# Up matmuls three slots ahead of the down matmuls instead of two, in a fused gated-EMA block and mixture of experts

## The reference

```
# layer 1, per batch
ctx   = ema(x, tau_ctx);  gated = x * sigmoid([x, ctx] @ Wg.T + bg)
mod   = 0.5 + sigmoid(gelu(x @ Wn1.T + bn1) @ Wn2.T + bn2)         # [t, 8]
trace_d = ema(gated * mod[:, d], tau_d), d = 0..7;  temporal = sum_d trace_d * softmax(blend)_d
gate  = sigmoid(temporal @ Wtemp.T + btemp);  soma = gelu(x @ Wsoma.T + bsoma)
x = x + layernorm((soma * gate) @ Wout.T) * gamma + beta
# layer 2, per batch: 3 shared dense blocks, 2 of 4 experts picked by the batch's type
dense(x, wi, wo) = relu(x @ wi) @ wo                               # wi 256x1024, wo 1024x256
s0, s1, s2 = dense(x, shared);  e = wa * dense(x, expert a) + wb * dense(x, expert b)
g = softmax(relu([e, s0, s1, s2](token 0) @ gate_w1) @ gate_w2)
x = x + g0 * e + g1 * s0 + g2 * s1 + g3 * s2
```

## Time and profile before

| | us |
|---|---|
| median of 3 runs | 1072.47 (1072.46 to 1073.15) |
| the profiled execution | 1071.64 |
| its span | 1070.1 |
| TensorE matmul busy | 1049.0 (98%) |
| VectorE busy | 767.1 (72%) |
| ScalarE busy | 398.4 (37%) |
| granted TensorE clock, mean | 0.998 of full |

### The profile page before, as it was taken

One profiled execution on the slowest core, in us unless ns is written; L12 is line 12 of the kernel. 1 busy time (PEld: TensorE's weight loads), 2 busy tenths in 40 slices (PEclk: granted clock), 3 DMA queues, 4 the chain that ended last, 5 costly groups with the idle time before them and its releaser, 6 DMA issues.

```text
span 1070.1 us, 12753 instructions
## 1 busy us (share of the span) xinstructions
PE 1049.0 (98%) x4870; PEld 861.0 (80%) x4870; DVE 767.1 (72%) x1269; ACT 398.4 (37%) x640; POOL 8.9 (1%) x20
## 2 busy tenths in 40 slices
PE   7799999999999999999999999999999999999998
PEld 5388777888788888888888888888888888888898
DVE  7979987499655995469864797539965499545236
ACT  6454445422333333432344323442233323323232
POOL 0000001000000000000000000000000000000000
PEclk9999999999999999999999999999999999999999
DMA  6359888676354574546644565445645456355582
GB/s 221 115 198 411 300 324 308 239 285 267 134 189 158 197 262 141 186 158 252 220 157 158 178 238 195 176 157 213 249 146 181 158 205 246 140 198 195 198 321 91
DMA packets 38142, 223.80 MB, mean 209 GB/s; under 512 B 4482, under 2 KB 5250, under 8 KB 16450
## 3 DMA queue, kind: packets, MB, share of 16 engines
q1 hardware_dynamic: 35778, 210.42, 54.5%
q0 software_dynamic: 2304, 12.58, 3.1%
HBM read 189.30 MB, written 33.69 MB: 208 GB/s over the span
## 4 chain that ended last, share of the span: by engine, by line
PE 57%; DVE 40%; issue 2%; ACT 1%; DMA 0%; DVEq 0%
DVE trace L1234 10%; DVE hid_lo L1124 8%; PE ps_up L646 7%; PE ps_up L653 7%; PE ps_up L647 7%; PE ps_down L684 7%; PE ps_down L685 7%; PE ps_down L688 7%; DVE trace L1265 6%; DVE temporal L1274 4%; PE ps_aux L615 4%; PE ps_aux L617 3%; PE ps_aux L616 3%; DVE x L1193 2%; DVE temporal L1234 1%
## 5 line engine op out<-in xcount | busy, mean ns | idle before, releaser
L1124 DVE SCALAR_TENSOR_TENSOR hid_lo<-ps_up,hid_hi 128x512 fp32r<-128x512 f32 (+1 forms) x336 | 219.7, 657 | 250.4 <-ACT hid_hi L925 248.9
L925 ACT ACTIVATE hid_hi<-ps_up 128x512 fp32r<-128x512 f32 (+1 forms) x336 | 193.7, 577 | 531.7 <-PE ps_up L653 531.5
L646 PE MATMUL ps_up<-x_hi_all,wi 128*128 128x512 f32 (+1 forms) x660 | 252.5, 384 | 0.7 <-DVE wi L1115 0.4
L647 PE MATMUL ps_up<-x_hi_all,wi 128*128 128x512 f32 (+1 forms) x660 | 249.9, 381 | 0.0
L684 PE MATMUL ps_down<-hid_hi,wo 128*128 128x512 f32 (+1 forms) x640 | 245.5, 385 | 0.2
L685 PE MATMUL ps_down<-hid_hi,wo 128*128 128x512 f32 (+1 forms) x640 | 245.1, 384 | 0.0
L653 PE MATMUL ps_up<-x_lo_all,wi 128*128 128x512 f32 (+1 forms) x660 | 197.4, 380 | 0.0
L688 PE MATMUL ps_down<-hid_lo,wo 128*128 128x512 f32 (+1 forms) x640 | 194.2, 385 | 1.7 <-DVE hid_lo L1124 1.7
L646 PEld LDWEIGHTS ps_up<-x_hi_all,wi 128*128 128x128 f32 x660 | 124.1, 188 | 25.0 <-DVE wi L1115 0.8
L647 PEld LDWEIGHTS ps_up<-x_hi_all,wi 128*128 128x128 f32 x660 | 124.1, 188 | 23.3
L653 PEld LDWEIGHTS ps_up<-x_lo_all,wi 128*128 128x128 f32 x660 | 122.1, 188 | 24.0 <-DVE x_lo_all L1115 0.2
(11 more groups left out here) (235 smaller groups left out, 875.8 us busy)
## 6 DMA issues: line engine op xcount, KB each, us to landing
wi<-split_wi SPq DMA_DIRECT2D x70, 1024.0 KB, 4.9
wo<-split_wo SPq DMA_DIRECT2D x70, 1024.0 KB, 4.9
modb<-mod_scratch SPq DMA_DIRECT2D x28, 512.0 KB, 4.4
split_wi<-wi SPq DMA_DIRECT2D x10, 1024.0 KB, 7.9
split_wo<-wo SPq DMA_DIRECT2D x10, 1024.0 KB, 8.2
xt<-in_x SPq DMA_DIRECT2D x8, 512.0 KB, 6.2
split_wi<-ex POOLq DMA_DIRECT2D x4, 1024.0 KB, 8.8
split_wo<-ex POOLq DMA_DIRECT2D x4, 1024.0 KB, 7.1
```

The costliest lines, as they stand in the source:

```text
L646: pe.matmul(ps, w_hi, x2_hi[:, parity, c, tokens], start=c == 0, stop=False)
L647: pe.matmul(ps, w_lo, x2_hi[:, parity, c, tokens], start=False, stop=False)
L925: act.activation(hid_hi[:, k % NU, tokens], ps_up[k % NU][:, tokens], ACT.Relu).then_inc(hid_hi_ready, 1)
L1124: dve.scalar_tensor_tensor(hid_lo[:, k % NU, tokens], ps_up[k % NU][:, tokens], 0.0, f32(hid_hi[:, k % NU, tokens]), ALU.max, ALU.subtract ...
```

## The change

`LAG` goes from 2 to 3; the relu and relu_lo of the opening follow it; and SyncE's `load_wi` for later batches moves from slot 4m+2 to slot 4m+1. Nothing else is edited: the plans, the places of `wi_round` and `wi_rest` in batch 0, and the number of buffers stay. Through `LAG` the opening issues three up groups per half, and the first up group of the next batch is issued in slot 37 instead of 38.

```
-LAG = 2
+LAG = 3
...
-                if k % 4 == 2 and not (last and m + 2 >= UNITS) and unit_of(b, m + 2)[0] > 0:
+                if k % 4 == 1 and not (last and m + 2 >= UNITS) and unit_of(b, m + 2)[0] > 0:
                     load_wi(b, m + 2)
...
-            relu(0, 0)
-            relu(0, 1)
+            for k in range(LAG):
+                relu(0, k)
...
-            relu_lo(0, 0)
-            relu_lo(0, 1)
+            for k in range(LAG):
+                relu_lo(0, k)
             wi_rest(1)
```

## The result

| | before | changed |
|---|---|---|
| median of 10 runs, us | 1072.3 | 1074.9 |
| lowest to highest | 1071.49 to 1073.15 | 1073.88 to 1075.71 |
| profiled execution, us | 1071.64 | 1074.43 |
| its span | 1070.1 | 1072.9 |

The ratio is 1.0024 with a 95% interval of 1.0015 to 1.0034: +2.6 us, between +1.6 and +3.6. A second series gave 1.0026 (1.0016 to 1.0036).

What follows compares the result with a forecast made beforehand. TensorE, busy 98%, bounds the kernel, with VectorE's backlog setting its waits in batch 0. Tgate's +2.09 less the opening's 0.68 gives +1.41: 1073.05 profiled, plus 0.83 for the median, 1073.9 us; range 1071.3 to 1075.8.

Steps and rivals of the forecast that it cites:

- The bound: Whole kernel: TensorE busy for 98% of the span; in batch 0 VectorE's backlog, 68.90 of 68.90 us, sets the waits.
- The opening: Before the loop: a third half group covers the wait for x2_hi and x2_lo; gain 0.68 us, bounds 0 and 0.76.
- The split of unit 1: Batch 0, slot 1: the low half of wi unit 1, ready at 69.66, just fits before 69.74.
- The wi waits: Batch 0: TensorE waits for late wi splits, 0.64 at slot 13, 0.8 to 0.9 each for units 5 and 6, 3.2 at slot 25.
- tgate: Batch 0, behind slot 26: begins 2.09 us later, set by TensorE, with ct_lo ready 0.3 us before; +1.41 with the opening.
- rival C: Batch 0, slot 25: the 3.2 us wait lowers TensorE's clock, costing 1.7 us more, 1075.6 us; chance 8%.
- a digit under 9 in the clock row: The page's clock row: a digit under 9 there would show the forecast wrong.
- The other batches: Batches after batch 0: same work and ct_lo waits stay; cost 0, bounds -0.1 and +0.1 us per batch.
- The wi loads: SyncE's queue, later batches: loads keep four slots (10.9 us) from release to use, no longer behind modb; cost 0.
- The bunching: Wi loads issued 1.4 us behind wo loads: two landings one after the other, 9.8 us, stay inside 10.9; cost 0.
- The last batch: The tail: TensorE waits for nothing there, and last matmul, last add and store keep their order; cost 0.
- rival D: Six batches: bunched transfers landing over 10.9 us make TensorE wait where units begin, +6 us, 1080; chance 5%.

Runs made afterwards that it cites:

- e10: e1 with modb2 and modb3 moved behind the wi loads in SyncE's queue (slots 10.5 and 14.5); 1074.54 us, 1.0025 of before.
- e9: Changed kernel with twelve matmuls of ones in front of slot 25 of batch 0, during TensorE's wait; 1074.16 us, 1.0016 of before.
- c2: The kernel of e9 run again, beside the changed kernel on the same chip; 1074.87 us, 1.0023 of before.
- e1: Changed kernel with the wi loads of later batches left in SyncE's slot 4m+2, lead of three kept; 1082.11 us, 1.0097 of before.
- e3: Changed kernel with 24 matmuls of ones in front of slot 25 of batch 0, during TensorE's wait; 1077.16 us, 1.005 of before.
- e2: Kernel before, lead of two, with only the wi loads of later batches moved to SyncE's slot 4m+1; 1072.21 us, 0.9999 of before.
- e4: Changed kernel with every wi split of batch 0 one slot earlier on ScalarE and VectorE; 1071.16 us, 0.9989 of before.

## Why the prediction came out as it did

The time lay in the range and at its upper half: forecast 1073.9, measured 1074.9; the loss, 2.6 us, is near double the 1.41 forecast. Against the prediction's own steps:

1. The bound. Right: VectorE's backlog decides batch 0, before through ct_lo and now through unit 7's split, and nothing that the lead removes from TensorE's waits there comes out as time.
2. The opening, 0.68 us net of the half groups' extra. Measured as 0.71 us less 0.08, which is 0.63. The split of unit 1 fitted, as written: slot 1 begins with no wait.
3. The wi waits. Forecast in front of slots 13, 17, 21 and 25, of 0.64, 0.87, 0.8 and 3.2 us from slot to slot. Measured are 0.45, 0.69, 0.57 and 2.99 idle; by the starts of the slots it is 0.74, 0.98, 0.86 and, in e10, where no fall of the clock hides it, 3.31. Each is 0.1 us over the forecast, and 0.3 over its idle row. No wait for unit 3. hid_lo gone.
4. tgate. Counted from slot 0, and without a fall of the clock (e9, c2, e10), it begins 2.09 to 2.11 us later than before, where +2.09 was forecast, and ct_lo was in time: tgate has no wait. It hangs on the time of unit 7's split, so the 0.1 us of the earlier waits don't add up in it.
5. The clock. This is the step that failed in the weighing, not in the mechanism. It stood as rival C at 8%, with the price of 1.7 us from the opening's row; the profile of the changed kernel has it, at 1.6 us, and so have four of five profiles with that wait. It should have been a term of the sum with a chance of about one half. 1.41 + 1.6 is 3.0 against 2.8 in the profiled execution; the executions without a fall lie 1.8 (changed) and 1.9 us (e10) over before, the others 2.8 and 3.1, and the median's 2.6 is between. Size and place of the price were right, but its source was not a good one: the low stretch of the opening, from which I took it, costs before nothing that its executions show (VectorE is busy for all of that stretch). The sign that I named for it, a digit under 9 in the clock row of the page, didn't come: a slice of that row is 27 us long, and the changed kernel has nines throughout; only a narrow window shows the fall. The Trainium skill (TensorE: Matmul & The Clock Gate, What's actually happening) states that the throttled clock is the default and activity releases it. This trace agrees, with 0.50 behind a 3 us wait, and e10 adds that the same wait can pass without a fall.
6. The other batches, 0. Measured within 0.2 us into batch 2, and each tgate from there to batch 6 starts 3.9 to 4.0 us later than before (2.8 were forecast; with 1.6 for the clock and 0.3 for the earlier start of the loop that is 4.1), so nothing is added on the way; ct_lo there waits as before (1.4 instead of 1.0 in batch 1, with no drift).
7. The wi loads, 0. Right as a sum over the whole change, wrong as an account of the edit. I saw that modb no longer stands in front of the load and gave it no price; without it the lead would cost 7.2 us more (e1, e10).
8. The bunching. Landings of wi went from 4.9 to 7.2 us, half of the way to the 9.8 that I had allowed, and the longest, 11.9, is beyond the 10.9 of cover. The last batch I had passed over in one line. Its slots have half of the tokens, so the cover there is shorter too: e3's wait of 1.10 us is a load issued at 1031.48 and used at 1039.26. It may be rival D on a small scale: it stands in one of the eleven profiles with a lead of three. The Trainium skill (Trainium Kernel Development and Optimization, Key Constraints) states that transfers of all queues run on the same 16 DMA engines and interleave. The trace fits it, with 7.2 against 4.9 us for the second load of a pair; but both loads of a pair come from SyncE's queue, and the first keeps its 4.8, so sharing between queues isn't tested here.

## What to carry to other kernels

A deeper lead moves the deadline of everything that feeds the leading stage; list the producers whose places in their queues stay, and find the one whose lateness is paid last. Here it was a single split out of ten. A wait of TensorE that grows in one piece costs more than its length: two short waits of before were 0.4 and 0.45 us of idle time, the single one of 3 us brought a stretch of half clock with it, 1.6 us more by slot 28, in four of five profiles. And an issuing queue passes on every wait in it: a transfer behind another's semaphore wait is late by that wait, which only shows when the slack is spent.

## What the runs showed of the hardware beyond that

A 1 MB load issued one up group (1.4 us) behind another of the same size lands after 7.2 us at the median instead of 4.9, while the first of the two stays at 4.8. A matmul of plain f32 with 128 columns is recorded as two and took 0.23 us in e3 (24 in 5.52 us), as long as one of the split type with 512 columns (0.227). And the granted clock of the same stretch of the opening, 24 to 38 us, was 0.88 in the profiles of before, changed, e2, e3 and e4 and 1.00 in the nine others, though no edit touches what stands ahead of it.
